# Stores reordered, features rectified on GpSimd, and the largest weight spread by TensorE, in a four-layer graph network

## The chip, the cores and the metric

One core of one Trainium2 chip runs the whole program. The metric is the device time in microseconds (us) of one execution, the median over several runs. The engines are TensorE (PE, whose weight loads are listed as PEld), VectorE (DVE), ScalarE (ACT), GpSimd (POOL) and SyncE (SP, which here only issues transfers).

## The reference, cut to what matters

4096 nodes with 256 features, an adjacency matrix of zeros and ones (4096 x 4096), four graph layers, each on the rectified layer norm of x and each added to x:

```python
h = jnp.maximum(_layernorm(x), 0.0)
# layer 0:  A = adj + I; A = A * dinv[:, None] * dinv[None, :]
x = x + leaky_relu(A @ concatenate([h[:2048] @ weightr, h[2048:] @ weightd]) + bias, 0.01)
h = jnp.maximum(_layernorm(x), 0.0)
# layer 1:  twice  h = relu(concatenate([h, adj @ h], axis=1) @ W)
x = x + h
# layer 2:  x + relu((a_norm @ h) @ W.T + b)
# layer 3:  x + elu(concatenate([attention @ h, -attention' @ h], axis=1) @ wtrans)
```

## The kernel before, in words

Nodes stand in eight chunks of 512 rows, a chunk in four tiles of 128. The adjacency arrives as 128 pieces of 512 KB, 16 for each chunk (GROUPS = 16), in turns n = 0 to 127. The text calls one pass of the loops over n on ScalarE and on VectorE a turn; both engines walk the turns in order, each at its own pace.

**The opening (layer 0, first part).** In turn n a piece is cast to bytes: by ScalarE, or, where n % 4 is 3, by VectorE (`by_act`). VectorE adds the bytes up to degrees (`count`, one piece a turn), ends a chunk's counts in the turn after its last piece (`counted`, turns 16, 32, ...), and computes mean and variance of the feature tiles (`x_stats`, STATS_AHEAD turns ahead; `means` after a chunk's four). ScalarE rectifies one feature tile a turn into a ring of four (`h0_tile`, from turn FIRST_TILE = 2). TensorE walks q = 0 to 16, two tiles a q: it transposes them (`h0_transposed(q)`, L1660), and multiplies the pair before by the weights (`y0(q-1)`, L1671). Between the two, ScalarE copies the transposed pair out of PSUM in turn 2q + 4 (`h0_t_copy`), and VectorE copies the product out in turn 2q + 7 (`y0_copy`, L1175). Before q = 7 and q = 15 TensorE needs the counts of chunk 0 and of chunk 1 (`degree_sums`, L1651, released by `counted`). After q = 16 it multiplies by the adjacency (`early_product`, `rest_product`, both L1593), in an order written out by hand, up to the end of layer 0. The largest weight, a scale, is reduced over the partitions by GpSimd (`largest`, L641); a second such reduction stands between the two products of layer 1.

**The end of layer 0.** Chunk by chunk, `linear` (DVE), `leaky` (ACT), `residual` (POOL, L649), statistics (DVE), `rectified` (ACT, L845 and L848) and `low` (POOL, L664) run, with the residual of chunk c + 1 between the tiles of chunk c; such a stretch for one c is called a block. The rectified chunk goes to memory from a ring of two slots (`store_h`), so `rectified(c)` waits until the store of chunk c - 2 has landed (`h_out`). SyncE issues in program order:

```python
for c in range(NC - 1):
    store_x(c)
    if c + 3 < NC:
        refill(c, c % 2, c // 2)
    if c > 0:
        store_h(c - 1)
load_weights(1)
store_h(NC - 2)
for c in range(NC - 1):
    reload(l, c)
```

`refill(c)` waits for the landing of `store_x(c)` and for `hi_ready` of chunk c, the last tile of `rectified(c)`, and then loads x for chunk c + 3. `reload(0)` brings chunk 0 of the rectified features back; the first product of layer 1 (L1733) waits for it.

Of the kernel before, what the change touches and what calls it, by code (L numbers as in the profile page):

```python
# [24 lines left out]
def gnn_stack(nc, x_in, adj_t, adj, w_gcn, b_gcn, w_conv1, w_conv2, w_gcn2, b_gcn2,  # L25
# [26 lines left out]
    SLOT = [0, 2, 6, 0, 2, 6, 4, 2]  # L52
    FIRST_TILE = 2
    STATS_AHEAD = 4
    RESTARTED = {2: 0, 3: 1, 4: 2, 5: 3, 7: 5}
# [14 lines left out]
    with ctx:  # L70
# [128 lines left out]
        def deg_ps(c):  # L199

            if c < 2:
# [8 lines left out]
        bias_in, part_ready, rect_ready, cols_ready = (sem("bias_in"), sem("part_ready"), sem("rect_ready"),  # L210
                                                       sem("cols_ready"))
        dsc0_ready, low_done = sem("dsc0_ready"), sem("low_done")
        small_in, weights_in = sem("small_in"), sem("weights_in")
# [26 lines left out]
        hs_ready, hi_ready, post_done = sem("hs_ready"), sem("hi_ready"), sem("post_done")  # L240
        gown_ready, gall_ready = sem("gown_ready"), sem("gall_ready")

# [70 lines left out]
        def by_act(n):  # L313

            return n % 4 != 3

        def casts_of(n):

            return n // 4 * 3 + n % 4 + 1 if by_act(n) else n // 4 + 1

        def act_casts(n):

            return n // 4 * 3 + min(n % 4, 3)

        def dve_casts(n):

            return n // 4

# [30 lines left out]
        def _(sp):  # L359
# [85 lines left out]
            for l in range(4):  # L445
# [48 lines left out]
                if l == 0:  # L494
                    for c in range(NC - 1):
                        store_x(c)
                        if c + 3 < NC:
                            refill(c, c % 2, c // 2)
                        if c > 0:
                            store_h(c - 1)  # L500
                    load_weights(1)
                    store_h(NC - 2)
                    for c in range(NC - 1):
                        reload(l, c)
                    store_x(NC - 1)
# [123 lines left out]
        def _(pool):  # L629
# [7 lines left out]

            def largest(n):

                pool.wait_ge(gown_ready, n + 1)  # L640
                nc.gpsimd.partition_all_reduce(g_all, g_own, P, bass.bass_isa.ReduceOp.max).then_inc(gall_ready, 1)  # L641

# [7 lines left out]

            largest(0)
            pool.wait_ge(bias_in, 16)
# [14 lines left out]
            for c in range(NC):  # L667
# [4 lines left out]
                if c == NC - 2:  # L672
                    for t in range(TPC):
                        low(c, t)
            largest(1)

# [7 lines left out]
        def _(act):  # L684
# [10 lines left out]
            def h0_tile(n):  # L695

                c, t = n // TPC, n % TPC
                if t == 0:
                    act.wait_ge(lncol_ready, c + 1)
                if t % 2 == 0:  # L700
                    wait(act, h0_t_ready, n // 2 - 1)
                nc.scalar.activation(h0_ring[:, t, :], x_all[c][:, t, :], ACT.Relu,
                                     bias=minus_mean[:, c % 4, t:t + 1]).then_inc(h0_done, 1)

# [29 lines left out]
            for n in range(PIECES):  # L734
                c, g = n // GROUPS, n % GROUPS
                if by_act(n):
                    if n == 4 * GROUPS:
                        act.wait_ge(lncol_ready, NC)
                        act.wait_ge(h0_done, NT)
# [292 lines left out]
        def _(dve):  # L1032
# [50 lines left out]
            values, roots, inverses = (load_cols[:, k, :, :] for k in range(3))  # L1083

            def largest_weight():

                dve.wait_ge(weights_in, 16)
                nc.vector.tensor_reduce(y_scale, w_sb, AX.XY, ALU.max)
                ch.link(nc.vector.tensor_reduce(y_inv, w_sb, AX.XY, ALU.min))
                ch.link(nc.vector.scalar_tensor_tensor(g_own, y_inv, -1.0, y_scale, ALU.mult, ALU.max))  # L1090
                nc.vector.tensor_scalar(g_own, g_own, 1e-30, None, ALU.max).then_inc(gown_ready, 1)

            def weight_scale():

                dve.wait_ge(gall_ready, 1)
                ch.link(nc.vector.tensor_scalar(g_pow.bitcast(i32), g_all.bitcast(i32), 0x7F800000, None,
# [69 lines left out]
            def means(c):  # L1166
                wait(dve, h0_done, (c - 3) * TPC)
                nc.vector.tensor_scalar(minus_mean[:, c % 4, :], x_mv[:, c, :, 0], -1.0, None, ALU.mult)\
                  .then_inc(lncol_ready, 1)
# [15 lines left out]
            for n in range(PIECES):  # L1185
# [14 lines left out]
                if not by_act(n):  # L1200
                    if n == 4 * GROUPS + 3:
                        dve.wait_ge(lncol_ready, NC)
                        dve.wait_ge(h0_done, NT)
                    if n in (6 * GROUPS + 3, 7 * GROUPS + 3):
# [44 lines left out]
            for l in range(4):  # L1249
                if l == 2:  # L1250
# [4 lines left out]
                    nc.vector.tensor_scalar(g_own, g_own, 1e-30, None, ALU.max).then_inc(gown_ready, 1)  # L1255
                    dve.wait_ge(gall_ready, 2)
                    ch.link(nc.vector.tensor_scalar(g_pow.bitcast(i32), g_all.bitcast(i32), 0x7F800000, None,
# [314 lines left out]
        def _(pe):  # L1572
# [82 lines left out]
            def h0_transposed(q):  # L1655
                pe.wait_ge(h0_done, 2 * q + 2)
                wait(pe, h0_t_evac, q - 1)
# [6 lines left out]
            def y0(q):  # L1664
# [8 lines left out]
                ins.then_inc(y0_ready, 1)  # L1673

            for q in range(PAIRS + 1):
# [18 lines left out]
            for m in range(REST):  # L1694
                rest_product(m)

            def spread(out_, column):

                return mm(out_, column.to_broadcast([P, P]), ident32[:, :], start=True, stop=True,  # L1699
                          skip_group_check=True)  # L1700

# [14 lines left out]
            for l in range(1, 4):  # L1716
# [183 lines left out]
```

## Time and profile before

| | us |
|---|---|
| median of 3 runs | 2111.86 (2110.57 to 2112.67) |
| the profiled execution | 2112.05 |
| its span | 2110.3 |
| TensorE busy | 2052.6, 97% of the span |
| VectorE, ScalarE, GpSimd busy | 1326.5, 1012.9, 53.6 |
| mean granted TensorE clock | 0.994 |

The profiled execution's own time is 1.8 us over its span and 0.2 us over the median. TensorE carries 90% of the chain that ended last, so a change of the time is a change of TensorE's waits or of its clock.

### The profile page before, as it was taken

To read this page: it belongs to the slowest core of one execution; us is meant where nothing else is said; L and a number is where in the kernel's file an instruction comes from. 1 tells how busy PE (TensorE), PEld (TensorE's weight loads), DVE (VectorE), ACT (ScalarE), POOL (GpSimd) and SP (SyncE) were. 2 spreads that over 40 slices of the span, in tenths; PEclk is the share of its full clock that TensorE was granted. 3 is DMA by queue.
4 is the path that set the end of the run, shared out by engine and by line. 5 is a ranking of instruction groups with operands and counts; after the bars stand their busy time and mean duration, and the time that the engine had idled before them with its cause. 6 is when DMAs were issued, how large, how long until landed. Compare 5 with 4: busy or idle time off the path is not lost.

```text
span 2110.3 us, 26133 instructions
## 1 busy us (share of the span) xinstructions
PE 2052.6 (97%) x10560; PEld 1493.7 (71%) x10560; DVE 1326.5 (63%) x2040; ACT 1012.9 (48%) x1333; POOL 53.6 (3%) x88
## 2 busy tenths in 40 slices
PE   5999989999999999999999899999999999999998
PEld 4888865555545555554555588888888888888887
DVE  6855440000044242434548899999999999999674
ACT  6755440000020000001104679797888788787873
POOL 0011340000000000000000000000000000000000
PEclk9999999999999999999999999999999999999999
DMA  9997352010311223301157645444445444351200
GB/s 376 381 349 278 111 202 48 21 41 21 100 50 56 65 64 96 117 31 61 48 109 313 170 160 207 138 180 145 180 144 179 165 140 180 132 212 65 100 20 11
DMA packets 102393, 288.25 MB, mean 137 GB/s; under 512 B 45184, under 2 KB 52096, under 8 KB 85760
## 3 DMA queue, kind: packets, MB, share of 16 engines
q1 hardware_dynamic: 96896, 278.19, 38.3%
q10 hardware_dynamic: 5376, 8.39, 1.3%
q8 instruction: 83, 1.36, 0.3%
q14 instruction: 38, 0.31, 0.0%
HBM read 245.11 MB, written 33.06 MB: 132 GB/s over the span
## 4 chain that ended last, share of the span: by engine, by line
PE 90%; DVE 3%; DMA 2%; ACT 2%; POOL 1%; issue 1%; SPq 0%; ACTq 0%; POOLq 0%; DVEq 0%
PE ps L1822 41%; PE ps L1733 32%; PE ps L1593 7%; PE ps L1750 7%; PE ps L1792 2%; DMA h_spill<-work 1%; POOL work L649 1%; PE ps L1699 1%; DMA feat<-in_adj 1%; PE ps L1671 1%; PE ps L1660 1%; ACT big L686 0%; DMA big<-in_adj_t 0%; POOL work L664 0%; DVE feat L1426 0%
## 5 line engine op out<-in xcount | busy, mean ns | idle before, releaser
L1733 PE MATMUL ps<-big,feat 128*128 128x512 fp8e4 x3072 | 671.1, 381 | 11.3 <-DMA feat<-h_spill 7.1
L1733 PEld LDWEIGHTS ps<-big,feat 128*128 128x128 f16 x3072 | 301.4, 98 | 375.0 <-issue 12.9
L1822 PE MATMUL ps<-big,work 128*128 128x257 f32 x2048 | 450.9, 381 | 4.9 <-ACT work L961 4.9
L1822 PE MATMUL ps<-big 128*128 128x257 f32 x2048 | 449.4, 380 | 3.5 <-ACT big L961 3.5
L1822 PEld LDWEIGHTS ps<-big,work 128*128 128x128 f32 x2048 | 388.4, 190 | 60.8 <-issue 4.8
L1822 PEld LDWEIGHTS ps<-big 128*128 128x128 f32 x2048 | 388.3, 190 | 59.6 <-ACT big L961 4.4
L1593 PE MATMUL ps<-feat,big 128*128 128x256 f16 x2048 | 224.7, 273 | 0.0
L1593 PEld LDWEIGHTS ps<-feat,big 128*128 128x128 fp8e4 x2048 | 199.9, 98 | 23.4
L686 ACT ACTIVATE big<-big 128x2048 bf16<-128x2048 f32 (+1 forms) x124 | 182.3, 1487 | 13.2 <-DMA big<-in_adj_t 12.9
L953 ACT ACTIVATE big<-feat,uv_sb 128x512 f32<-128x512 f32 x256 | 163.3, 710 | 22.5 <-PE ps L1822 22.5
L953 ACT ACTIVATE work<-feat,uv_sb 128x512 f32<-128x512 f32 x256 | 163.4, 713 | 16.5 <-PE ps L1822 15.8
L691 ACT ACTIVATE ln<-ln 128x4 f32<-128x4 f32 x24 | 4.9, 205 | 338.4 <-DVE ln L1057 338.4
L1278 DVE TENSOR_REDUCE gmax<-work 128x1 f32<-128x256 f32 x32 | 11.9, 414 | 244.6 <-ACT work L813 244.6
L1507 DVE TENSOR_TENSOR big<-big,feat 128x2048 f32<-128x2048 f32 x64 | 146.3, 2286 | 29.4 <-ACT big L953 20.8
L1507 DVE TENSOR_TENSOR work<-work,feat 128x2048 f32<-128x2048 f32 x64 | 146.3, 2286 | 22.9 <-ACT work L953 19.1
L961 ACT ACTIVATE big<-big 128x2048 f32<-128x2048 f32 x64 | 122.0, 1906 | 72.1 <-DVE big L1523 71.5
L961 ACT ACTIVATE work<-work 128x2048 f32<-128x2048 f32 x64 | 122.1, 1908 | 68.4 <-DVE work L1523 68.3
L1523 DVE TENSOR_TENSOR work<-work,big 128x2048 f32<-128x2048 f32 x64 | 146.3, 2287 | 0.5
L1523 DVE TENSOR_TENSOR big<-big 128x2048 f32<-128x2048 f32 x64 | 146.1, 2282 | 0.5
L1750 PE MATMUL ps<-work 128*128 128x256 f32 x640 | 142.4, 379 | 2.6 <-ACT work L686 2.6
L1750 PEld LDWEIGHTS ps<-work 128*128 128x128 f32 x640 | 121.4, 190 | 22.1 <-ACT work L686 3.8
L686 ACT ACTIVATE work<-ps 128x1024 f32<-128x1024 f32 (+1 forms) x43 | 35.8, 831 | 208.1 <-PE ps L1733 202.2
(165 smaller groups left out, 1365.9 us busy)
## 6 DMA issues: line engine op xcount, KB each, us to landing
big<-in_adj_t SPq DMA_DIRECT2D x64, 1024.0 KB, 4.9
feat<-in_adj SPq DMA_DIRECT2D x56, 1024.0 KB, 6.9
big<-in_adj_t SPq DMA_DIRECT2D x80, 512.0 KB, 9.6
h_spill<-work SPq DMA_DIRECT2D x31, 512.0 KB, 3.6
feat<-h_spill SPq DMA_DIRECT2D x31, 512.0 KB, 4.7
work<-in_adj_t SPq DMA_DIRECT2D x27, 512.0 KB, 6.7
x_spill<-work SPq DMA_DIRECT2D x24, 512.0 KB, 2.7
feat<-in_adj_t SPq DMA_DIRECT2D x21, 512.0 KB, 8.6
```

Of the source, the lines that this page charges most:

```text
L649: nc.gpsimd.tensor_tensor(x_t, hs32[:, t % 2, :], x_t, ALU.add).then_inc(residual_added, 1)
L686: return nc.scalar.activation(out_, in_, ACT.Copy, **kw)
L953: ins = nc.scalar.activation(slots[:, t, :], AB[:, 2 * (c % 2), :], ACT.Prelu, bias=uv_sb[:, j, 1:2], alpha=ALPHA)
L961: nc.scalar.activation(slots, slots, ACT.Exp, scale=1.0 if k < QPH else -1.0).then_inc(p_ready, 1)
L1507: nc.vector.tensor_tensor(slots, slots, AB[:, 2 * s + 1:2 * s + 2, :].to_broadcast([P, QD, CH]), ALU.subtract).then_inc(shifted, 1)
L1523: nc.vector.tensor_tensor(slots, slots, mask[:, q * QD:(q + 1) * QD, :], ALU.add if s == 0 else ALU.subtract).then_inc(lin_ready, 1)
L1593: ins = mm(ps[:, bank + t // 2, (t % 2) * F:(t % 2 + 1) * F], adj_units[:, i, j0 + jj, t * P:(t + 1) * P], parts[:, j0 + jj, h, :], start= ...
L1660: ins = mm(h0_t(q)[:, t, k, :], h0_ring[:, (2 * q + t) % TPC, k * P:(k + 1) * P], ident32[:, :], start=True, stop=True, skip_group_check=True)
L1733: ins = mm(ps[:, bank + f, :], parts[:, j, h, f * P:(f + 1) * P], adj_units[:, c, j, :], start=(fresh and h == 0), stop=(end and h == 1), ...
L1750: ins = mm(out_slot(t), T_sb[:, k, t * P:(t + 1) * P], w_sb[:, k, :], start=(k == 0), stop=(k == KB[l] - 1), skip_group_check=True)
L1792: ins = mm(ps[:, 4 + j % Y_BANKS, :], T_all[:, c, k, t * P:(t + 1) * P], wt_sb[:, k, :], start=(k == 0), stop=(k == FB - 1), skip_group_ch ...
L1822: ins = mm(ps[:, 4 * s + t, 0:YW], quads[k % RING][:, jj, t * P:(t + 1) * P], Yb[:, j, s, :], start=(j == 0), stop=(j == NT - 1), skip_gro ...
```

## The change

1. SyncE issues `store_h(c - 1)` ahead of `refill(c)` instead of behind it.
2. Only the four tiles of chunk 0 are rectified by ScalarE, in turns 0 to 3; the 28 others by GpSimd, each as one instruction (add, then max), released by `means` and by the ring. ScalarE casts all pieces of turns 0 to 31.
3. FIRST_TILE goes from 2 to 0: `h0_t_copy(q)` moves to turn 2q + 2 and `y0_copy(q)` to turn 2q + 5. STATS_AHEAD goes from 4 to 3: `means(c)` moves from turn 4c - 1 to turn 4c. `rows_of_a` moves from q = 6 to q = 5, its copy from turn 17 to 14.
4. The reduction over partitions becomes a TensorE product with the identity, which spreads the 128 partial maxima along a row (`spread_largest`), and a VectorE maximum over that row (`largest`). This stands at q = 6, where VectorE needs it in turn 15, and behind the last projection of the first product of layer 1.

```diff
-    FIRST_TILE = 2
-    STATS_AHEAD = 4
+    FIRST_TILE = 0
+    STATS_AHEAD = 3
         def by_act(n):
-            return n % 4 != 3
+            return n < 2 * GROUPS or n % 4 != 3
...
                         store_x(c)
+                        if c > 0:
+                            store_h(c - 1)
                         if c + 3 < NC:
                             refill(c, c % 2, c // 2)
-                        if c > 0:
-                            store_h(c - 1)
...
-            def largest(n):
-                pool.wait_ge(gown_ready, n + 1)
-                nc.gpsimd.partition_all_reduce(g_all, g_own, P, bass.bass_isa.ReduceOp.max).then_inc(gall_ready, 1)
+            def h0_tile(n):
+                c, t = n // TPC, n % TPC
+                if t == 0:
+                    pool.wait_ge(lncol_ready, c + 1)
+                if t % 2 == 0:
+                    wait(pool, h0_t_ready, n // 2 - 1)
+                nc.gpsimd.tensor_scalar(h0_ring[:, t, :], x_all[c][:, t, :], minus_mean[:, c % 4, t:t + 1], 0.0,
+                                        ALU.add, ALU.max).then_inc(h0_done, 1)
...
-            largest(0)
+            for n in range(TPC, NT):
+                h0_tile(n)
...
-            largest(1)
...
-                if FIRST_TILE <= n < FIRST_TILE + NT:
-                    h0_tile(n - FIRST_TILE)
+                if n < TPC:
+                    h0_tile(n)
...
-                if n == 17:
+                if n == 14:
...
+            def largest(n):
+                dve.wait_ge(g_spread, n + 1)
+                ch.link(nc.vector.tensor_reduce(g_all, ps[:, 4 * n, 0:P], AX.X, ALU.max))
...
+                if n == 0:
+                    pe.wait_ge(hsc_ready, 1)
...
+            def spread_largest(n):
+                pe.wait_ge(gown_ready, n + 1)
+                spread(ps[:, 4 * n, 0:P], g_own).then_inc(g_spread, 1)
...
             for q in range(PAIRS + 1):
+                if q == 6:
+                    spread_largest(0)
...
-                if q == 6:
+                if q == 5:
                     rows_of_a()
...
+                if l == 1:
+                    spread_largest(1)
```

## Rows read from the trace of the kernel before

**Rows 1.** Window of a stage: busy of PE, PEld, DVE, ACT, POOL; PE clock, DMA.

```profile
77.00:297.80 220.80, 220.80 (x2041) 197.53 (x2038) 118.57 (x397) 121.98 (x208) 47.85 (x71) 1.00 0.68 249
```

**Rows 2.** Timeline of PE, layer 0 into 1: start, us, line, what, idle before.

```profile
304.89 44.06 PE L1733 MATMUL ps<-big,feat 128*128 128x512 fp8e4 x192 [7.07 <-DMA feat<-h_spill]
```

**Rows 3.** Window of 2 us behind the gap, columns as in group 1.

```profile
306.00:308.00 2.00, 2.00 (x6) 0.76 (x5) 0.78 (x2) 2.00 (x6) 0.00 (x0) 0.50 1.03 420
```

**Rows 4.** The chain that ended last, in order of time: start, us, what.

```profile
299.42 5.33 DMA feat<-h_spill
...
869.92 41.44 PE ps L1733 x192
```

**Rows 5.** Timeline of ACT: the first rectified tile of blocks 2, 5 and 6.

```profile
251.64 0.60 ACT L845 ACTIVATE work<-work,ln 128x256 f32<-128x256 f32 x1 [3.27 <-DMA h_spill<-work]
...
285.44 0.60 ACT L845 ACTIVATE work<-work,ln 128x256 f32<-128x256 f32 x1 [5.08 <-DMA h_spill<-work]
...
294.13 0.60 ACT L845 ACTIVATE work<-work,ln 128x256 f32<-128x256 f32 x1 [1.24 <-DVE ln L1399]
```

**Rows 6.** Timeline of SP's issues: store_x(1), refill(1), store_h(0).

```profile
238.46 0.33 SPq L455 DMA_DIRECT2D x_spill<-work  x1
245.94 0.33 SPq L399 DMA_DIRECT2D work<-in_x  x1
246.32 0.43 SPq L463 DMA_DIRECT2D h_spill<-work  x1
```

**Rows 7.** Timeline of PE in the opening: q = 1, 6, 12 and the last two products.

```profile
19.68 2.07 PE L1660 MATMUL ps<-ident,work 128*128 128x128 f32 x8 [2.03 <-ACT work L702]
21.55 2.70 PE L1671 MATMUL ps<-work 128*128 128x256 f32 x8
...
44.86 2.99 PE L1671 MATMUL ps<-work 128*128 128x256 f32 x8
...
60.57 1.05 PE L1660 MATMUL ps<-ident,work 128*128 128x128 f32 x8
...
73.38 3.62 PE L1671 MATMUL ps<-work 128*128 128x256 f32 x16
```

**Rows 8.** Timeline of DVE in the opening.

```profile
42.72 0.43 DVE L1135 CAST work<-acc 128x512 bf16<-128x512 uint8 x1
...
58.09 0.17 DVE L1168 TENSOR_SCALAR minus_mean<-x_mv 128x4 f32<-128x4 f32 x1
...
64.14 0.41 DVE L1163 BATCH_NORM_STATS2 stat<-big 128x6 f32<-128x256 f32 x1
...
64.80 0.17 DVE L1168 TENSOR_SCALAR minus_mean<-x_mv 128x4 f32<-128x4 f32 x1
...
67.22 0.69 DVE L1208 CAST big<-feat 128x1024 uint8<-128x1024 f32 x1
67.82 0.69 DVE L1175 COPY work<-ps 128x512 f32<-128x512 f32 x1
68.42 0.95 DVE L1117 TENSOR_TENSOR acc<-acc,big 128x512 uint16<-128x512 uint16 x2
...
69.73 0.43 DVE L1135 CAST work<-acc 128x512 bf16<-128x512 uint8 x1
```

**Rows 9.** Group by shape of DVE, 0 to 80 us: busy us, mean ns, idle.

```profile
L1117 DVE TENSOR_TENSOR acc<-acc,big 128x512 uint16<-128x512 uint16 x34 | 14.4, 423 | 1.7 <-ACT big L686 0.7
```

**Rows 10.** Groups by shape of POOL, whole span.

```profile
L649 POOL TENSOR_TENSOR work<-work 128x256 f32<-128x256 f32 x32 | 23.2, 727 | 72.0 <-ACT work L765 72.0
...
L635 POOL TENSOR_SCALAR_AFFINE_SELECT ident<-ident 128x128 f32<-128x128 f32 x1 | 0.3, 282 | 0.0
```

**Rows 11.** Timeline of DVE while POOL adds four tiles without a break (113.8 to 116.9 us).

```profile
115.56 0.74 DVE L1117 TENSOR_TENSOR acc<-acc,big 128x512 uint16<-128x512 uint16 x1
```

**Rows 12.** The chain that ended last, between the two products of layer 1.

```profile
586.67 0.17 DVE sc L1255
...
587.38 0.17 DVE sc L1257
```

More of the change, by code:

```diff
@@ L211, in gnn_stack @@
                                                        sem("cols_ready"))
+        h0_first = sem("h0_first")
         dsc0_ready, low_done = sem("dsc0_ready"), sem("low_done")
@@ L240, in gnn_stack @@
         hs_ready, hi_ready, post_done = sem("hs_ready"), sem("hi_ready"), sem("post_done")
-        gown_ready, gall_ready = sem("gown_ready"), sem("gall_ready")
+        gown_ready, g_spread = sem("gown_ready"), sem("g_spread")
         ht_ready, ht_evac = sem("ht_ready"), sem("ht_evac")
@@ L313, in by_act @@
         def by_act(n):
-            return n % 4 != 3
+            return n < 2 * GROUPS or n % 4 != 3
         def casts_of(n):
-            return n // 4 * 3 + n % 4 + 1 if by_act(n) else n // 4 + 1
+            return sum(by_act(m) == by_act(n) for m in range(n + 1))
         def act_casts(n):
-            return n // 4 * 3 + min(n % 4, 3)
+            return sum(by_act(m) for m in range(n))
         def dve_casts(n):
-            return n // 4
+            return sum(not by_act(m) for m in range(n))
         def piece_slot(n):
@@ L699, in h0_tile @@
                     act.wait_ge(lncol_ready, c + 1)
-                if t % 2 == 0:
-                    wait(act, h0_t_ready, n // 2 - 1)
                 nc.scalar.activation(h0_ring[:, t, :], x_all[c][:, t, :], ACT.Relu,
-                                     bias=minus_mean[:, c % 4, t:t + 1]).then_inc(h0_done, 1)
+                                     bias=minus_mean[:, c % 4, t:t + 1]).then_inc(h0_first, 1)
             def h0_t_copy(q):
@@ L738, in _ @@
                         act.wait_ge(lncol_ready, NC)
-                        act.wait_ge(h0_done, NT)
+                        act.wait_ge(h0_first, TPC)
+                        act.wait_ge(h0_done, NT - TPC)
                     if n in (6 * GROUPS, 7 * GROUPS):
@@ L1093, in weight_scale @@
             def weight_scale():
-                dve.wait_ge(gall_ready, 1)
+                largest(0)
                 ch.link(nc.vector.tensor_scalar(g_pow.bitcast(i32), g_all.bitcast(i32), 0x7F800000, None,
@@ L1166, in means @@
             def means(c):
-                wait(dve, h0_done, (c - 3) * TPC)
+                if c >= 4:
+                    dve.wait_ge(h0_first, TPC)
+                    wait(dve, h0_done, (c - 4) * TPC)
                 nc.vector.tensor_scalar(minus_mean[:, c % 4, :], x_mv[:, c, :, 0], -1.0, None, ALU.mult)\
@@ L1202, in _ @@
                         dve.wait_ge(lncol_ready, NC)
-                        dve.wait_ge(h0_done, NT)
+                        dve.wait_ge(h0_first, TPC)
+                        dve.wait_ge(h0_done, NT - TPC)
                     if n in (6 * GROUPS + 3, 7 * GROUPS + 3):
@@ L1255, in _ @@
                     nc.vector.tensor_scalar(g_own, g_own, 1e-30, None, ALU.max).then_inc(gown_ready, 1)
-                    dve.wait_ge(gall_ready, 2)
+                    largest(1)
                     ch.link(nc.vector.tensor_scalar(g_pow.bitcast(i32), g_all.bitcast(i32), 0x7F800000, None,
@@ L1655, in h0_transposed @@
             def h0_transposed(q):
-                pe.wait_ge(h0_done, 2 * q + 2)
+                if q < 2:
+                    pe.wait_ge(h0_first, 2 * q + 2)
+                else:
+                    pe.wait_ge(h0_done, 2 * q + 2 - TPC)
                 wait(pe, h0_t_evac, q - 1)
@@ L1673, in y0, with spread @@
                 ins.then_inc(y0_ready, 1)
+            def spread(out_, column):
+                return mm(out_, column.to_broadcast([P, P]), ident32[:, :], start=True, stop=True,
+                          skip_group_check=True)
+            def spread_largest(n):
+                pe.wait_ge(gown_ready, n + 1)
+                spread(ps[:, 4 * n, 0:P], g_own).then_inc(g_spread, 1)
             for q in range(PAIRS + 1):
+                if q == 6:
+                    spread_largest(0)
                 if q in (7, 15):
@@ L1695, in _ @@
                 rest_product(m)
-            def spread(out_, column):
-                return mm(out_, column.to_broadcast([P, P]), ident32[:, :], start=True, stop=True,
-                          skip_group_check=True)
             def transposed(c):
```

## The prediction

> **What bounds the kernel now.** I read the page's engine shares first: TensorE is busy 97% of the span, and its line is most of the chain. So I asked for its waits and its timeline. After the opening, from 77.0 to 297.8 us, it never waits [rows 1]; behind it comes the longest wait of the whole trace, 7.07 us before the first product of layer 1, ended by the transfer that brings the rectified chunk 0 back [rows 2]. The chain says when that transfer was issued: at 299.42 us, landing 5.3 us later [rows 4], and SyncE issues it behind `store_h(6)`, which waits for GpSimd's last `low` of chunk 6. The gap costs more than itself. In the 2 us window behind it the granted clock is 0.50, that is 1.2 instead of 2.4 GHz [rows 3]; the 192 products there take 44.06 us, the 192 of layer 2 at full clock 41.44 [rows 2, 4]. Gap and clock together are 7.07 + 2.62 = 9.69 us. Then I read the timelines of ScalarE and SyncE for the blocks before it, and those of TensorE and VectorE for the opening. These two places, and one between the products of layer 1, are what the change touches.
>
> **The reordered store.** Block 2 starts its first rectified tile after an idle of 3.27 us that a store ends, block 6 after 1.24 us that only its own columns end [rows 5]. The store in question is `store_h(0)`: SyncE issued `store_x(1)` at 238.46, then stood at `refill(1)` until 245.94, and only then, at 246.32, the store [rows 6]. Moved ahead of the refill it goes out right behind `store_x(1)`, nearly 8 us earlier, and has landed before block 2 asks. Nothing is put behind a longer wait: refill(c) waits for the last tile of block c, and by then the store's own condition (the residuals of chunk c, which `store_x(c)` has waited for already) is long met; the x load that it issues is needed two blocks later. The four blocks that wait for a store idle 3.27, 3.22, 3.17 and 5.08 us; each falls to 1.24 (two of the four are in [rows 5]). That is 2.03 + 1.98 + 1.93 + 3.84 = 9.8 us. One limit appears: `linear(4)` needs products that TensorE ends at 259.3 us (its 50 rest products end at 297.8 us [rows 1] and take 1.75 us each, and the 28th is the last that it needs), about 1 us after block 3 would like it. So the last `low` of chunk 6 moves from 298.98 to about 290.1, the reload from 299.42 to 290.5, landing at 295.8. TensorE asks at 297.8. The gap closes with 2.0 us to spare, and with it the low clock behind it: -9.7 us.
>
> **Between the products of layer 1.** GpSimd's reduction sits between the VectorE instructions at 586.67 and 587.38, that is 0.54 us from the end of one to the start of the other [rows 12]. In its place come a hand-over to TensorE, one f32 product, a hand-over back and a VectorE maximum over 128 values in PSUM. At least: 0.5, for nothing gained. At most: 0.25 for a small product with its hand-overs doubled, and 0.4 for a maximum, some 1.1 us. I take 0.8, so +0.25 us. It lies on TensorE's path, which waits there before and after.
>
> **The opening: what it gets.** VectorE loses eight casts of 0.60 us each from start to start (67.22 to 67.82 in [rows 8]); ScalarE takes them and loses 28 rectified tiles. DMA is nearly full in this stage whatever the order. What counts is when TensorE ends its last two `y0` products, at 77.0 us [rows 7]; from there it is never short of work. VectorE is the paced engine, so I lay its instructions end to end with the steps of rows 8: statistics of a tile 0.66 (64.14 to 64.80), a count 0.34 to 0.49, taken 0.34 in a mixed turn, a `y0_copy` 0.60, `means` 0.1.
>
> *To q = 7.* The first `y0_copy` is now in turn 5. TensorE can deliver: pair 1 after four tiles, from 17.0 us, 2.07 for the transposes, 2.5 to 2.7 for the product [rows 7], so 21.5 us, and VectorE waits. Then turns 5 to 9 cost three copies, five statistics, five counts, the diagonal's 0.65 and a `means`: 7.5 us. Turn 10, with the largest weight, 3.65. Turns 11 to 16 three copies, six statistics, six counts, two `means`, the scale with its new maximum 1.05, `counted` 0.8: 9.85. Sum 42.5 us for `count_ready`, against 42.72 + 0.43 = 43.15 before [rows 8]. The 1.2 us of casts that lay in this stretch have gone into the wait at turn 5.
>
> *q = 7 to 12.* TensorE has by then run out of pairs some 4 us earlier. It does the degree sums, the transposes of q = 7 and y0(6), at low clock as before (2.99 us at 44.86, against 3.62 for the two last products together, [rows 7]), and ends at 47.1. Before, VectorE in turn 17 copied y0(5), which was long there. Now turn 17 copies y0(6), and so waits until 47.1. Its rest (0.6 + 0.66 + 0.34), turn 18 (1.0), the square roots that ScalarE gives at 50.2 after its copy of q = 8 and a table load, the columns (1.5), turn 19 (1.8) and turn 20 (1.35) bring it to 54.9 us. Turns 21 to 23 are three statistics, three counts, three `y0_low` of 0.4 and two copies, 5.4 us; turn 24's statistics and `means(6)` end at 61.05, against 58.26 [rows 8]. GpSimd then rectifies two tiles before q = 12 can be transposed. For one tile no row exists: the nearest are 0.282 us for a 128x128 select and 0.727 for a two-operand add of the same size [rows 10]; between them I take 0.5. That gives 62.2 against 60.57 [rows 7]: +1.6.
>
> *q = 12 to the end.* Before, TensorE went from 60.57 to 77.0 without a pause: 16.4 us. Now one appears. `degree_sums(1)` at q = 15 needs `counted` of turn 32, and before it VectorE must copy y0(13) in turn 31, which TensorE has only just finished. Copy, two counts, the fold and the cast took from 67.82 to 70.16 [rows 8]: 2.4 us in which TensorE stands. End: 62.2 + 16.4 + 2.4 = 81.0, +4.0. The adjacency products behind have what they need: relative to that end, the last `y0_copy` comes 2.4 us after it and is asked for at 3.5; the second tile pair of chunk 1 comes 6.9 after and is asked for at 8.75.
>
> **The shared path of VectorE and GpSimd.** While GpSimd added four tiles without a break, a VectorE count took 0.74 us [rows 11] against a mean of 0.423 [rows 9]: +0.32 for a meeting. Now GpSimd has 28 tiles in the stretch where VectorE has 28 counts; at 0.5 us a tile it is busy some 30% of it, so 8 or 9 meetings, 2.7 us, of which I take the part that falls on the path and not into VectorE's waits: +1.0. The Trainium skill, "SBUF — State Buffer", section "Who interferes with whom", states why: the second port pair is an exclusive lock, taken by GpSimd or by a VectorE instruction with two SBUF inputs for its whole length, and the other "fully blocks". By that rule the count that meets a tile waits for all the rest of it, which the trace agrees with (0.74 against 0.42); it gives the second rival below.
>
> **Sum.** -9.7 + 0.25 + 4.0 + 1.0 = -4.45 us. The profiled execution took 2112.05, its span 2110.3; the median is 0.2 us lower, so from the median 2111.86 - 4.45 = 2107.4 us. Bounds: the opening could cost between 1.5 less than nothing (the eight casts less the wait) and 9; the closed gap gives between 5 and 9.7; the spread costs 0 to 0.6.
>
> **Rivals.**
> - *The opening costs nothing* (chance 0.20). If TensorE delivers y0(0) and y0(6) sooner than I lay it out, because ScalarE has lost 28 tiles, the two turns' head start shows and cancels the pause at q = 15: 2111.9 - 9.7 + 0.25 = 2102.4 us, up to 2104. For it: ScalarE was 80 to 100% busy there. Against it: VectorE sets the pace.
> - *The port* (0.15). GpSimd's tile costs 0.73 like its add, and all meetings lie on the path: three rounds with two tiles each, 3 x 2 x 0.23 = 1.4, and 2.1 more of meetings: 2107.4 + 3.5 = 2110.9 us, within 0.2%.
> - *The gap does not close* (0.06). The store was not what held the blocks back, or `low` of chunk 6 slips by more than 2.0 us: then TensorE waits again and the clock falls again. With half of the 9.7 us gone: 2112.2 us, no change. Here the reordering would not do what it can.
> - *Slower* (0.09): one tile on GpSimd takes 1.5 us or more. Its place is between `means(c)` and the transposes of q = 2c, in five rounds, c = 3 to 7, once it is so long; each then costs two tiles. At T us a tile that adds 2 x 5 x (T - 0.5). At 1.5 us it is 10 us and the time 2117.4; the sign turns at about 0.95 us a tile. For it: no row of this instruction. Against: the adds of the same size take 0.727 us [rows 10].
> - *My forecast* (0.50), with a range of its own from 2105.4 to 2109.4.
>
> The Trainium skill, "GPSIMD Engine Reference", section "4.1 Engine selection", calls one-input elementwise work on GpSimd roughly line-rate; no run here shows it yet, and it would speak for the short end of my 0.28 to 0.73.
>
> **Numbers.** About 0.2% (4.2 us) is what a measurement of this kernel can tell from no change, so the line lies at 2107.6, inside my forecast. Faster: 0.27 of the forecast's 0.50, and the first rival's 0.20: 0.47. Same: 0.23 + 0.15 + 0.06 = 0.44. Slower 0.09. Range for 8 in 10: 2102.0 to 2112.0, which leaves out the slower rival.
>
> **What would show it.** Right: no idle ahead of L1733's first product, and 192 of them in 41.4 us; blocks 2 to 5 idle 1.24 us; the last `y0` product ends near 82 us; TensorE waits at q = 7 for some 4 us and at q = 15 for over 2. Wrong: the opening ends at 77 or before; the product of layer 1 still waits for h_spill; GpSimd tiles over 0.8 us; VectorE counts that stay at 0.42.

## The result, and the profile after

| | before | after |
|---|---|---|
| median, us | 2111.77 (2110.57 to 2112.67) | 2120.07 (2118.27 to 2121.66) |
| span of the profiled execution | 2110.3 | 2119.5 |
| last `y0` product ends | 77.00 | 94.46 |
| first product of layer 1 starts | 304.89 | 315.84 |

The ratio is 1.004 (95% interval 1.0028 to 1.0051): slower by 8.3 us, where the forecast was faster by 4.5. The gap at layer 1 did close; the opening took the gain back twice over.

The gap first. The timeline of TensorE at the boundary of layers 0 and 1 [rows 2]; then, of ScalarE, the first tile of block 2 [rows 5]; then SyncE's issues of `store_x(1)`, `store_h(0)`, `refill(1)` and the reload [rows 6].

```profile
226.76 89.24 PE L1606 MATMUL ps<-feat,big 128*128 128x256 f16 x816
315.84 14.41 PE L1758 MATMUL ps<-big,feat 128*128 128x512 fp8e4 x66
```

```profile
267.79 0.60 ACT L850 ACTIVATE work<-work,ln 128x256 f32<-128x256 f32 x1 [1.23 <-DVE ln L1412]
```

```profile
256.65 0.33 SPq L456 DMA_DIRECT2D x_spill<-work  x1
257.28 0.33 SPq L464 DMA_DIRECT2D h_spill<-work  x1
264.14 0.33 SPq L400 DMA_DIRECT2D work<-in_x  x1
...
308.54 4.32 SPq L417 DMA_DIRECT2D feat<-h_spill  x7
```

The store now follows `store_x` after 0.6 us and no longer stands behind the refill. All seven blocks idle 1.23 or 1.24 us, for their own columns (one row shown). The reload goes out 7.3 us before TensorE asks (290.5 against 297.8 in the prediction, 7.3 too), and the first product follows 816 others without a wait.

Now the opening. The timeline of TensorE from q = 4 (the first two rows) and from q = 6, rows at waits and at low clock [rows 7]:

```profile
29.93 1.16 PE L1678 MATMUL ps<-ident,work 128*128 128x128 f32 x8 [2.98 <-POOL work L646]
30.93 1.89 PE L1689 MATMUL ps<-work 128*128 128x256 f32 x8
...
38.02 1.77 PE L1678 MATMUL ps<-ident,work 128*128 128x128 f32 x8 [1.47 <-POOL work L646]
39.59 2.99 PE L1689 MATMUL ps<-work 128*128 128x256 f32 x8
46.48 0.26 PE L1666 MATMUL ps<-ones,work 128*128 128x1 bf16 x4 [3.90 <-DVE work L1145]
...
48.45 3.62 PE L1689 MATMUL ps<-work 128*128 128x256 f32 x8
...
62.08 1.92 PE L1678 MATMUL ps<-ident,work 128*128 128x128 f32 x8 [4.72 <-POOL work L646]
63.79 2.84 PE L1689 MATMUL ps<-work 128*128 128x256 f32 x8
...
72.34 1.94 PE L1678 MATMUL ps<-ident,work 128*128 128x128 f32 x8 [3.09 <-POOL work L646]
...
88.06 0.25 PE L1666 MATMUL ps<-ones,work 128*128 128x1 bf16 x4 [2.44 <-DVE work L1145]
...
89.15 5.31 PE L1689 MATMUL ps<-work 128*128 128x256 f32 x16
```

TensorE starts 5.5 us earlier than before (its first transpose at 10.07 us, against 15.61) and then stands again and again. Behind the five pauses from 38.02 on it runs slow: eight products take 2.8 to 3.6 us where 1.89 is the full-speed value, and the last 16 take 5.31, before 3.62. Behind the pause of 2.98 us at 29.93 it did not: 1.89 us, as the second row shows. The granted clock of two such stretches, and of one between them (windows, columns as in [rows 1]; 0.50 is 1.2 GHz throughout, 0.58 has some of the stretch at 2.4):

```profile
48.50:51.50 3.00, 3.00 (x9) 2.37 (x9) 0.00 (x0) 2.49 (x3) 2.26 (x2) 0.50 1.00 396
52.00:57.00 5.00, 5.00 (x33) 4.59 (x31) 4.04 (x17) 3.92 (x6) 0.00 (x0) 1.00 0.52 202
64.00:66.00 2.00, 2.00 (x6) 1.61 (x6) 0.00 (x0) 1.97 (x4) 0.74 (x1) 0.58 0.18 74
```

The groups of TensorE up to 94.4 us, first of before, then of after, say how much each part is (busy, mean ns, idle):

```profile
L1671 PE MATMUL ps<-work 128*128 128x256 f32 x128 | 32.0, 397 | 0.0
...
L1660 PE MATMUL ps<-ident,work 128*128 128x128 f32 x128 | 20.5, 310 | 22.0 <-ACT work L702 21.9
...
L1651 PE MATMUL ps<-ones,work 128*128 128x1 bf16 x12 | 0.7, 165 | 1.3 <-DVE work L1135 1.3
```

```profile
L1689 PE MATMUL ps<-work 128*128 128x256 f32 x128 | 38.0, 452 | 0.0
L1678 PE MATMUL ps<-ident,work 128*128 128x128 f32 x128 | 22.6, 333 | 26.7 <-ACT work L706 14.4 <-POOL work L646 12.3
...
L1666 PE MATMUL ps<-ones,work 128*128 128x1 bf16 x8 | 0.5, 168 | 6.3 <-DVE work L1145 6.3
```

Idle went from 23.3 to 33.0 us (+9.7), and the same products and transposes take 60.6 us busy instead of 52.5 (+8.1). Together 17.8, against 17.46 by which the opening ends later. Nearly half of the loss is low clock; 0.67 of the 8.1 us is the first eight products (3.37 us, before 2.70), where the windows read a granted clock of 1.00. The idle hides how much the pauses grew, since 15.6 us of it before and 10.1 after lie ahead of the first transpose: behind it they went from 7.7 to 22.9 us.

Why does it wait? The timeline of VectorE has the loop, in its `y0_copy` rows (L1187) and `means` rows (L1180) [rows 8]:

```profile
42.68 0.69 DVE L1187 COPY feat<-ps 128x512 f32<-128x512 f32 x1 [3.02 <-PE ps L1689]
...
45.99 0.43 DVE L1145 CAST work<-acc 128x512 bf16<-128x512 uint8 x1
...
52.11 0.69 DVE L1187 COPY feat<-ps 128x512 f32<-128x512 f32 x1 [4.69 <-PE ps L1689]
...
59.40 0.17 DVE L1180 TENSOR_SCALAR minus_mean<-x_mv 128x4 f32<-128x4 f32 x1
...
66.66 0.69 DVE L1187 COPY feat<-ps 128x512 f32<-128x512 f32 x1 [2.93 <-PE ps L1689]
...
69.35 0.17 DVE L1180 TENSOR_SCALAR minus_mean<-x_mv 128x4 f32<-128x4 f32 x1
...
76.92 0.69 DVE L1187 COPY work<-ps 128x512 f32<-128x512 f32 x1 [3.91 <-PE ps L1689]
...
79.46 0.17 DVE L1180 TENSOR_SCALAR minus_mean<-x_mv 128x4 f32<-128x4 f32 x1 [0.28 <-DVE x_mv L1174]
```

Read one round. `means(5)` at 59.40 lets GpSimd rectify two tiles; TensorE, which has run dry, starts q = 10 on them at 62.08 and ends y0(9), which stands behind those transposes, at 66.63; VectorE has been standing at turn 23 for that product and copies it at 66.66; only behind the copy come the last statistics and `means(6)`, at 69.35. Then it begins again: 9.95 us a round and 10.1 the next, where the rounds of before took 7.4 and 6.7 (50.71, 58.09, 64.80). Three engines work one after the other, and the adjacency pieces wait behind them.

The groups of GpSimd [rows 10] and of VectorE's counts [rows 9], for the two prices:

```profile
L646 POOL TENSOR_SCALAR work<-big,minus_mean 128x256 f32<-128x256 f32 x28 | 33.2, 1200 | 49.3 <-DVE minus_mean L1180 47.6 <-PE ps L1678 1.8
```

```profile
L1127 DVE TENSOR_TENSOR acc<-acc,big 128x512 uint16<-128x512 uint16 x32 | 14.1, 442 | 5.8 <-ACT big L692 5.0
```

Between the products of layer 1, the timeline of VectorE [rows 12]:

```profile
595.17 0.15 DVE L1268 TENSOR_SCALAR sc<-sc 128x1 f32<-128x1 f32 x1
595.90 0.29 DVE L1093 TENSOR_REDUCE sc<-ps 128x1 f32<-128x128 f32 x1 [0.58 <-PE ps L1695]
596.22 0.15 DVE L1270 TENSOR_SCALAR sc<-sc 128x1 int32<-128x1 int32 x1
```

From the end of the first row to the start of the last are 0.90 us, against 0.54.

### The profile page after: what moved, and what is told of

The parts are those of the page before. It is cut to its first block, busy times and chain, and to the rows that moved or that the text cites. A ratio compares the mean times of both kernels' runs of the same rounds, so it can differ in the third digit from the quotient of the medians.

```text
span 2119.5 us, 26138 instructions
## 1 busy us (share of the span) xinstructions
PE 2058.3 (97%) x10564; PEld 1500.7 (71%) x10564; DVE 1323.7 (62%) x2034; ACT 1009.7 (48%) x1313; POOL 86.2 (4%) x114
## 4 chain that ended last, share of the span: by engine, by line
PE 93%; DVE 3%; DMA 1%; ACT 1%; issue 1%; POOL 0%; SPq 0%; DVEq 0%; ACTq 0%
PE ps L1849 41%; PE ps L1758 31%; PE ps L1606 10%; PE ps L1775 6%; PE ps L1819 2%; PE ps L1689 1%; PE ps L1695 1%; DMA feat<-in_adj 1%; DMA work<-in_adj_t 1%; PE ps L1678 1%; POOL work L646 0%; DVE feat L1439 0%; DVE acc L1127 0%; ACT big L692 0%; DVE stat L1173 0%
## 5 line engine op out<-in xcount | busy, mean ns | idle before, releaser
L692 ACT ACTIVATE big<-big 128x1024 uint8<-128x1024 f32 (+1 forms) x130 | 188.0, 1467 | 8.7 <-DMA big<-in_adj_t 8.5
L958 ACT ACTIVATE big<-feat,uv_sb 128x512 f32<-128x512 f32 x256 | 163.3, 710 | 22.9 <-PE ps L1849 22.7
L697 ACT ACTIVATE ln<-ln 128x4 f32<-128x4 f32 x24 | 4.9, 205 | 337.5 <-DVE ln L1062 337.5
L1775 PEld LDWEIGHTS ps<-work 128*128 128x128 f32 x640 | 121.4, 190 | 22.1 <-ACT work L692 3.8
```

What stands on the lines that cost most here:

```text
L692: return nc.scalar.activation(out_, in_, ACT.Copy, **kw)
L958: ins = nc.scalar.activation(slots[:, t, :], AB[:, 2 * (c % 2), :], ACT.Prelu, bias=uv_sb[:, j, 1:2], alpha=ALPHA)
L1775: ins = mm(out_slot(t), T_sb[:, k, t * P:(t + 1) * P], w_sb[:, k, :], start=(k == 0), stop=(k == KB[l] - 1), skip_group_check=True)
```

## The experiments

Times are medians; each ratio is to the kernel before on the same chip. That kernel took 2111.8 us beside the changed one, 2110.5 beside (2) and beside (4) with late sums, and 2112.2 beside all others. The intervals are some 3 us to either side, so a step between two lines of under 3 us is not shown by the times, and one of 3 to 5 us has intervals that touch or overlap a little. "End" is where the last `y0` product ends.

| kernel | us | ratio (95% interval) | end, us |
|---|---|---|---|
| before | 2111.8 | | 77.00 |
| 1 before + stores reordered | 2101.94 | 0.9949 (0.9935 to 0.9964) | 77.41 |
| 2 and the new largest weight | 2103.73 | 0.9964 (0.9951 to 0.9978) | 77.75 |
| 3 and GpSimd tiles, casts on ScalarE | 2100.06 | 0.9941 (0.9926 to 0.9955) | 74.33 |
| 4 and STATS_AHEAD 3 | 2099.50 | 0.9944 (0.9929 to 0.9959) | 74.01 |
| after = 4 and FIRST_TILE 0 | 2120.07 | 1.004 (1.0028 to 1.0051) | 94.46 |

Each line has one part of the change more than the line above it, so the last step carries the loss. The other runs ask what in it does.

**The stores, alone and undone.** The new order in the kernel before (1), and the old order in the changed one:

```diff
                         store_x(c)
+                        if c > 0:
+                            store_h(c - 1)
                         if c + 3 < NC:
                             refill(c, c % 2, c // 2)
-                        if c > 0:
-                            store_h(c - 1)
```

> The kernel before with the reordered stores alone. If the gap before layer 1 and the low clock behind it are what that part is worth, as predicted: 2111.8 - 9.7 = 2102.1 us, no wait before the first product of layer 1. If the order of stores is worth nothing by itself and the gap closed in the changed kernel only because its opening is late: 2111.8 us, gap still 7 us.

> The changed kernel with the stores back in the old order. By the first theory the 9.7 us come back: 2120.1 + 9.7 = 2129.8 us. By the rival, in which the late opening hides the blocks: 2120.1 us.

Measured 2101.94 us, and 2129.96 (ratio 1.0081, 1.0066 to 1.0096): 10.3 won in the one (against its own 2112.2), 9.9 lost in the other, 9.7 predicted. The first product of layer 1, with the reordered stores alone and with the old order in the changed kernel (timelines of TensorE):

```profile
298.45 41.60 PE L1733 MATMUL ps<-big,feat 128*128 128x512 fp8e4 x192
```

```profile
323.20 44.15 PE L1758 MATMUL ps<-big,feat 128*128 128x512 fp8e4 x192 [7.09 <-DMA feat<-h_spill]
```

The gap is 7.09 us even when everything arrives 18 us later: it is made by the blocks' stores, not by where the opening ends. This part is settled, and does not interact with the rest.

**The tiles back on ScalarE**, in turn n, all else as changed:

```diff
-            for n in range(TPC, NT):
-                h0_tile(n)
...
-                if n < TPC:
+                if n < NT:
                     h0_tile(n)
```

> The changed kernel, but ScalarE rectifies all tiles, one a turn, with the new turns and all casts on ScalarE. Theory 1, the price of a GpSimd tile (1.2 us, against 0.5 assumed) and the low clock that its waits bring are the loss: the opening ends at about 80 us instead of 94.5, the time is near 2106 us. Theory 2, the new turns are the loss whoever rectifies (means two turns ahead instead of five, the pauses at q = 7 and 15): the opening still ends past 90 us, 2116 us or more. Theory 3, the shared port of VectorE and GpSimd: as theory 1 here, but VectorE's counts fall back from 0.441 to 0.42 us on average.

Measured 2117.0 us (ratio 1.0021, 1.0012 to 1.0031), end 89.67. Only 3.1 us came back: the loop runs through ScalarE just as well. (By the traces the end moved by 4.8, of which 1.7 is that the last 16 products ran at full speed here, 3.62 us, behind the same pause of 2.43.) The mean count fell from 442 to 423 ns, which is what GpSimd's work beside them costs the counts: 32 counts by 0.019 us, 0.6 us, where I had taken 1.0.

**The old turns**, (3) in the table:

```diff
-    FIRST_TILE = 0
-    STATS_AHEAD = 3
+    FIRST_TILE = 2
+    STATS_AHEAD = 4
```

> The changed kernel with FIRST_TILE = 2 and STATS_AHEAD = 4 as before, GpSimd still rectifying 28 tiles. If the loss is the tile's price only where nothing hides it, means five turns ahead cover two tiles of 1.2 us: the opening ends near 77 us and the time is 2111.8 - 9.7 + 0.3 = 2102.5 us or a little more. If GpSimd's price counts wherever it stands (ring of four, two tiles a pair): 2112 us or more. If the port is the loss: 2108 to 2112, with counts at 0.44 us or longer.

Measured 2100.06 us with GpSimd's tiles at 1204 ns each (1200 in the changed kernel). The same dear instruction, and 20 us less: its price by itself is not the cause.

**Half of each GpSimd tile** (128 of the 256 columns are left out of the rectification):

```diff
-                nc.gpsimd.tensor_scalar(h0_ring[:, t, :], x_all[c][:, t, :], ...
+                nc.gpsimd.tensor_scalar(h0_ring[:, t, 0:P], x_all[c][:, t, 0:P], ...
```

> The changed kernel, but GpSimd rectifies only the left 128 of the 256 columns of its 28 tiles (the other half of the features is left out there), so each instruction is shorter and all else is as it was. If a tile's time is what its columns cost, it falls from 1.20 to some 0.65 us. Theory price: two tiles stand in each of five rounds, so the opening gains 5 x 2 x 0.55 = 5.5 us and what the clock gives back, 2112 to 2115 us. Theory turns: VectorE's waits for TensorE stay, the opening gains 3 us or less, 2117 us or more.

Measured 2114.57 us (ratio 1.0008, 0.9999 to 1.0018), end 86.86, tiles 809 ns. So 0.39 us less a tile gave 5.5 us (7.6 by the ends in the traces). By the groups of TensorE its idle fell by 3.2 us (two tiles in each of five rounds would be 3.9) and its busy time on transposes and products, 56.2 against 60.6, by 4.4: shorter pauses, less low clock. In the loop the tile's price counts, out of it (above) it doesn't.

**One constant of the two.** Means back at turn 4c - 1, and FIRST_TILE back at 2, (4) in the table:

```diff
-    STATS_AHEAD = 3
+    STATS_AHEAD = 4
```

> The changed kernel with STATS_AHEAD = 4, so means(c) comes one turn earlier (4c - 1), and FIRST_TILE = 0 kept. If late means are what makes the new turns slow, means now end ahead of a y0_copy that waits: the opening gains 5 us or more, 2115 us or less. If the coupling of VectorE to TensorE through y0_copy is it: within 2 us of 2120.

```diff
-    FIRST_TILE = 0
+    FIRST_TILE = 2
```

> The changed kernel with FIRST_TILE = 2 and STATS_AHEAD = 3 kept: the copies go back to turns 2q + 4 and 2q + 7, means stay in turn 4c. If the copies' turns are the loss: the opening ends near 75 us as with both restored, 2101 us. If late means are: it ends past 85 us, 2110 us or more.

Measured 2113.45 us (ratio 1.0005, 0.9996 to 1.0015), end 85.52, and 2099.50, end 74.01. The first run by itself speaks for the late means, the second for the copies' turns, and both are right: with STATS_AHEAD = 4 `means(c + 1)` still stands behind the copy of y0(2c - 1), now in the same turn, so that only less work lies in a round (7.1 and 9.2 us, by the means at 54.68, 61.80 and 70.96 us); FIRST_TILE alone undoes 20.6 us. The next runs split it.

**Only VectorE's copy back at turn 2q + 7:**

```diff
-                q = (n - FIRST_TILE - 5) // 2
+                q = (n - 7) // 2
```

> The changed kernel with only y0_copy put back to turn 2q + 7; the transposed copies stay at 2q + 2 and means at 4c. If VectorE's waits for a product that TensorE has only just finished (3.0, 4.7, 2.9, 3.9, 1.3, 2.7 us in the changed kernel's opening) are the loss, most of 20 us comes back: 2103 us. If late means are: 2115 us or more, TensorE still waiting for GpSimd's tiles. If the transposed copies' turns are (ScalarE waiting 33 us for TensorE): 2115 us or more too, with those waits unchanged.

Measured 2106.0 us (ratio 0.9974, 0.9962 to 0.9985), end 78.69: 14.1 of the 20.6 us are this one line, and the interval is clear of both neighbours'. It opens the loop. In the changed kernel the copy of y0(2c - 1), which needs the tiles of chunk c, is in turn 4c + 3, ahead of `means(c + 1)` in turn 4c + 4; two turns later it is behind it. The timeline of VectorE in (4), same stretch of work:

```profile
54.87 0.17 DVE L1180 TENSOR_SCALAR minus_mean<-x_mv 128x4 f32<-128x4 f32 x1
...
55.68 0.68 DVE L1187 COPY feat<-ps 128x512 f32<-128x512 f32 x1
...
60.73 0.17 DVE L1180 TENSOR_SCALAR minus_mean<-x_mv 128x4 f32<-128x4 f32 x1
```

Of the 16 copies only the first and y0(13), at 65.15 us, wait (1.76 us; one that doesn't is shown), and a round takes 5.86 us instead of 10.1. TensorE's groups up to 77 us there:

```profile
L1689 PE MATMUL ps<-work 128*128 128x256 f32 x128 | 31.9, 396 | 1.1 <-ACT work L692 1.1
L1678 PE MATMUL ps<-ident,work 128*128 128x128 f32 x128 | 19.5, 300 | 18.1 <-ACT work L706 14.2 <-POOL work L646 3.8
```

The clock came back with it: 396 ns a product, where the changed kernel has 452.

The other 6.5 us are what is left between the two kernels: ScalarE's copy of the transposed pair, in turn 2q + 2 instead of 2q + 4. With it early, VectorE's columns of turn 19 wait for square roots that ScalarE takes only behind its own waits for TensorE (a copy at 42.33 us after an idle of 2.53, one more at 44.95); in (4) the same instruction stands at 43.75 without a wait. The timeline of VectorE with its own copy alone moved back:

```profile
47.10 0.20 DVE L1068 RECIPROCAL load_cols<-load_cols 128x8 f32<-128x8 f32 x1 [2.42 <-ACT load_cols L697]
```

That these 6.5 us all come by this wait is read from one trace, not tried.

**The copy later still**, (4) with turn 2q + 9:

```diff
-                q = (n - FIRST_TILE - 5) // 2
+                q = (n - 9) // 2
```

> FIRST_TILE back at 2, STATS_AHEAD 3, and VectorE's copy of a product two turns later still, in turn 2q + 9. If the copy's turn alone sets TensorE's waits, a little faster than 2099.5, by up to 1.5 us. If at turn 2q + 7 VectorE no longer waits for TensorE, nothing is left to gain: 2099 to 2100; if TensorE then runs out of free banks for its products, slower, 2101 to 2104.

Measured 2103.74 us (ratio 0.9962, 0.9948 to 0.9977), end 76.98: the third case, TensorE out of free banks. Its timeline:

```profile
49.62 1.97 PE L1689 MATMUL ps<-work 128*128 128x256 f32 x8 [0.60 <-DVE feat L1187]
...
53.04 1.97 PE L1689 MATMUL ps<-work 128*128 128x256 f32 x8 [0.56 <-DVE feat L1187]
```

So of the turns tried 2q + 7 is the best: earlier, VectorE waits for TensorE; later, TensorE for VectorE.

**The degree sums one q later**, in the changed kernel and in (4):

```diff
-                if q in (7, 15):
-                    degree_sums(q // 8)
+                if q in (8, 16):
+                    degree_sums(q // 8 - 1)
```

> The changed kernel with the degree sums at q = 8 and q = 16 instead of 7 and 15. If the two pauses of TensorE ahead of them (3.90 and 2.44 us) are lost time, about 2113 to 2115 us and both pauses gone or under 0.5 us. If the wait only moves to the products, which then wait for VectorE's copies as before, 2118 to 2120.

> FIRST_TILE 2 and STATS_AHEAD 3 as in the best kernel so far (2099.5 us), with the degree sums at q = 8 and 16 instead of 7 and 15. If the pause of 2.57 us that it still has ahead of the first sums is lost time, 2097 to 2098 us. If the tiles of GpSimd, for which TensorE waits 3.8 us behind it, set the end of the opening whatever stands before, 2099 to 2100.

Measured 2111.97 us (ratio 0.9999, 0.9989 to 1.0009), end 85.56: 8.1 us of the loss. I had expected 5 to 7. Between the sums and VectorE the same kind of loop stands: turn 17 waited 4.69 us for y0(6), which stood behind sums that waited 3.90 us for VectorE. At the good turns it was a miss on both counts: 2101.75 us (ratio 0.9954, 0.9942 to 0.9967), the interval overlapping that of (4), end 75.62 against 74.01. The pause is gone, but the last product then waits for a copy that VectorE makes only behind `counted` of turn 32:

```profile
73.65 1.97 PE L1689 MATMUL ps<-work 128*128 128x256 f32 x8 [1.42 <-DVE work L1187]
```

**ScalarE's tiles at good turns**: (4) with all 32 tiles on ScalarE, which also keeps all casts of turns 0 to 31.

```diff
-            for n in range(TPC, NT):
-                h0_tile(n)
...
-                if n < TPC:
-                    h0_tile(n)
+                if FIRST_TILE <= n < FIRST_TILE + NT:
+                    h0_tile(n - FIRST_TILE)
```

> FIRST_TILE 2 and STATS_AHEAD 3 as in the best kernel so far (2099.5 us), with the 28 tiles back on ScalarE, which also keeps all casts of turns 0 to 31. If moving the tiles to GpSimd is worth something, because ScalarE would be the later of the two, this is slower: 2101 to 2104. If the 1.2 us of a GpSimd tile costs as much as it saves, 2099 to 2100. If the tile's price still lies on the path at these turns, faster: 2096 to 2098.

Measured 2104.11 us (ratio 0.9964, 0.9951 to 0.9977), end 78.49. That is 4.6 us more than (4), and TensorE waits 25.3 us for ScalarE. But this run moves two things: the tiles of chunk 0, too, go from turns 0 to 3 back to turns 2 to 5, and TensorE starts at 16.28 us instead of 10.31. How much of the 4.6 us is GpSimd's work and how much the earlier start was not separated. Its ratio is that of (2), which has VectorE's casts of before: the times show no gain by the extra casts on ScalarE alone.

**The new largest weight alone**, (2) in the table: TensorE's spread and VectorE's maximum (and `rows_of_a` one q earlier) on top of the reordered stores, with the tiles, casts and turns of before.

```diff
...
-                    dve.wait_ge(gall_ready, 2)
+                    largest(1)
...
+                if q == 6:
+                    spread_largest(0)
...
+                if l == 1:
+                    spread_largest(1)
```

> The kernel before with the reordered stores and the largest weight found by TensorE and VectorE, and nothing else: no GpSimd tiles, the old turns, the old casts. Beside the kernel with the stores alone (2101.9 us). If the new reduction costs what the trace of the changed kernel shows between the products of layer 1 (+0.35 us) and nothing in the opening, 2102.0 to 2102.7. If TensorE's wait for the weights at q = 6, or VectorE's for TensorE in turn 15, lies on the path of the opening, 2103 to 2105.

Measured 2103.73 us, against 2101.94, with intervals that overlap; the kernel before took 2110.5 and 2112.2 beside them, so by the ratios the step is 3.2 us, and the median lies where the second expectation put it. The profiled spans are 2102.1 and 2101.4. By the traces the opening ends 0.34 us later and the boundary costs 0.36 (the next product starts at 581.17 against 580.56, of which 0.25 lie before). Its 192 products then took 44.31 us against 43.24, while the changed kernel's took 43.22: how the clock falls there isn't set by this edit. By the traces the new reduction has 0.7 us of the whole; what more the times show is not explained. Either way it is in (3) and (4) too, and no cause of a loss of 8.3.

**What the instruction costs alone.** Trial instructions on GpSimd in layer 1, in the kernel before, four of each form, on a scratch tile (its allocation and semaphore are left out here), in one execution:

```diff
...
+            turn(lambda o, a, b: ts(o, a, s1, 0.0, ALU.add, ALU.max), F)
+            turn(lambda o, a, b: ts(o, a, 0.5, 0.0, ALU.add, ALU.max), F)
+            turn(lambda o, a, b: ts(o, a, s1, None, ALU.add), F)
+            turn(lambda o, a, b: ts(o, a, 0.5, None, ALU.max), F)
+            turn(lambda o, a, b: ts(o, a, s1, 0.0, ALU.add, ALU.max), P)
+            turn(lambda o, a, b: ts(o, a, s1, 0.0, ALU.add, ALU.max), 64)
+            turn(lambda o, a, b: nc.gpsimd.tensor_tensor(o, a, b, ALU.add), F)
```

> The kernel before, with 28 trial instructions added on GpSimd in layer 1, four of each form, on a scratch tile, so that VectorE's work of the opening is not beside them. Theory 1, the instruction itself is dear: add and max with a column of scalars takes about 1.20 us for 256 columns here too, some 0.8 for 128, and the two-input add 0.73. Theory 2, it is VectorE beside it in the opening that stretches it: then about 0.7 us here. If the column of scalars is the price, the form with an immediate number is clearly shorter; if the second operation is, the forms with one operation are.

The groups of GpSimd, L691 to L697 in the order of the diff:

```profile
L691 POOL TENSOR_SCALAR work<-work 128x256 f32<-128x256 f32 x4 | 4.5, 1145 | 0.1
L692 POOL TENSOR_SCALAR work<-work 128x256 f32<-128x256 f32 x4 | 4.2, 1064 | 0.0
L693 POOL TENSOR_SCALAR work<-work 128x256 f32<-128x256 f32 x4 | 3.6, 924 | 0.0
L694 POOL TENSOR_SCALAR work<-work 128x256 f32<-128x256 f32 x4 | 3.3, 845 | 0.0
L695 POOL TENSOR_SCALAR work<-work 128x128 f32<-128x128 f32 x4 | 2.8, 715 | 0.0
L697 POOL TENSOR_TENSOR work<-work 128x256 f32<-128x256 f32 x4 | 2.8, 723 | 0.0
L696 POOL TENSOR_SCALAR work<-work 128x64 f32<-128x64 f32 x4 | 1.9, 499 | 0.0
```

The instruction itself is dear: 1.145 us alone, 1.20 in the opening. The second operation is worth 0.22 us, the column of scalars 0.08. From 64 to 128 columns it grows by 0.216 us, from 128 to 256 by 0.43, 3.4 ns a column in both, over a base of 0.28.

## Why the prediction was wrong, point by point

- **The reordered store: right, by its own steps.** -9.7 predicted, -10.3 (1 against before) and -9.9 (undone) measured; no gap, products at full clock, all blocks at 1.24 us. The reload's lead over TensorE's ask, 7.3 us, was the predicted one.
- **Between the products: +0.25 predicted, +0.36 measured.** A small mis-sizing of one term.
- **The opening: +4.0 predicted, +17.5 measured. This is the step that failed**, and the sentence that failed is the walk of VectorE "laid end to end". I gave VectorE a wait for TensorE at turns 5 and 17 (and 31), and wrote turns 21 to 23 as 5.4 us of work. But the copies of y0(5), y0(9) and y0(11), in turns 15, 23 and 27, waited too, 3.02, 2.93 and 3.91 us, for products that stand on TensorE behind tiles that VectorE's own last `means` had released three turns (some 7 us) before. I walked one engine forward and never asked whether what it waits for hangs on what it had just done. Undoing the copy's turn alone gave 14.1 us back. In the sum's own terms: y0(6) ended at 52.07 us, not 47.1; turns 21 to 23 took 8.4 us (60.24 to 68.68), not 5.4; q = 12 was transposed at 72.34, not 62.2; and the rest took 22.1 us, not 18.8. TensorE did start 5.5 us earlier, but (3) and (4) start at 10.86 and 10.31 us as well: that comes from ScalarE's first tiles in turns 0 to 3, not from the copies' turns.
- **A part of the same step: count_ready.** 42.5 predicted, 46.42 measured; 3.0 of the 3.9 us are turn 15's wait. The move of the degree sums shows that the two pauses there, 3.90 us and the 2.44 that I had put at 2.4, are the second loop, 8.1 us. The runs' shares (14.1, 8.1, 6.6, 5.5) don't add up, since each of them shortens the same rounds.
- **The low clock behind the pauses was left out.** I carried one slow stretch over "as before"; there were five, and with them most of the 8.1 us of added busy time in the opening's 17.5.
- **The GpSimd tile: 0.5 us taken, 1.20 measured**, above both ends of my bounds (0.28 and 0.73). The bounding rows were other instructions: an add of two tensors is no upper bound for an add and a maximum. The Trainium skill, "GPSIMD Engine Reference", section "4.1 Engine selection", calls one-input elementwise work roughly line-rate, and two-input work the slower. The runs do not bear it out, and the measurement decides: here the one-input form with two operations took 1.145 us, those with one operation 0.845 to 0.924, and the two-input add 0.723.
- **The rivals.** The slower one named the right place, five rounds between `means(c)` and q = 2c, and its formula with the measured 1.20 gives 2107.4 + 7.0 = 2114.4 us. Its cause was too narrow: at the old turns tiles of the same 1.20 us gave 2100.06. A chance of 0.09 hung on the tile's price; it belonged on the turns. The rival that the opening costs nothing failed for this kernel. Its 2102.4 us is near what the old copies' turns give (2099.5 and 2100.1), but it named a head start by the new ones, so that the numbers are close is luck.
- **The port: +1.0 predicted, 0.6 measured** in VectorE's counts, and not all of it on the path. No run shows the 2.1 us of further meetings that its rival added.

What stays open: why the first 192 products of layer 1's second half take 43.2 us in some kernels and 44.3 in others, behind the same wait of 2.44 us. Open too is when a pause costs TensorE its clock and when not. Nor was it tried whether the copy at turn 2q + 8 would gain.

The best version is the changed kernel with FIRST_TILE = 2: 2099.5 us, 0.9944 (0.9929 to 0.9959) of before. With STATS_AHEAD = 4 beside it, it is the same within the intervals.

## What to carry to other kernels

When an edit moves a consumer earlier in one engine's program, write down for each wait of that engine what the awaited result needs, back to the last instruction of the same engine in the chain. If that instruction stands shortly before the wait, the engines take turns instead of overlapping, and each microsecond of any of them counts in each round; the cure is to move the wait behind the next release (here one line, 14 us), not to speed the members up (half a tile, 5.5 us). And where TensorE pauses, look for slow stretches behind the pauses: here 15 us more of pauses came with 8 us more of busy time for the same products.

## What the runs showed of the hardware

- GpSimd's add-and-maximum over 128x256 f32 costs 1.145 us alone, 0.28 plus 3.4 ns a column; dropping one of the two operations saves 0.22, replacing the column of scalars by a number 0.08.
- The two-input adds beside it are cheaper at the same size: 0.723 us.
- With the partition reduction gone from the program, GpSimd's two selects start at 1.32 us instead of 11.50, where they had an idle of 10.4 us ahead of them with no releaser (with the stores alone reordered 11.04, with the new reduction as well 1.31). Nothing hung on them: with the new reduction alone TensorE starts at 15.76 us, as before.
- Short pauses can cost TensorE its clock, and need not: in the changed kernel eight products of 1.89 us took 2.82 to 3.62 behind pauses of 1.5 to 4.7 us, but 1.89 behind one of 2.98. Behind 2.4 us ahead of the second degree sums the last 16 took 5.31 there and 3.62 with half tiles; with the means one turn earlier a pause of 3.61 us left eight at 1.89, and one of 1.97 was followed by 3.51. The mean of all 128 went from 397 to 452 ns.
